# Source rows in a graph kernel: 2, 3, 2, 3 chunks per group fetched by TensorE, the rest gathered by GpSimd, in four passes over the edges

## The reference, cut to what matters

```python
# network 0, layer l
msg = h[src] * edge_weight[:, None]
h_neigh = segment_sum(msg, dst, num_segments=n) * inv_deg
h = h @ W_self[l].T + h_neigh @ W_neigh[l].T + b_neigh[l]
# network 1, layer l (h was scaled by norm_out)
m = h[src] * (a_mu + exp(a_ls) * eps)      # eps: 64 numbers for each edge
agg = segment_sum(m, dst, num_segments=n)
h = agg * norm_in @ W + b
```

## Time and profile before

| | us |
|---|---|
| runs, median of 3 | 11286.28 (11276.57 to 11294.67) |
| profiled execution, time | 11292.81 |
| its span | 11291.0 |
| mean granted TensorE clock | 0.711 of full speed |
| TensorE matmul busy | 7355.7 (65%) |
| VectorE busy | 7439.4 (66%) |
| GpSimd busy | 5284.9 (47%) |
| ScalarE busy | 3043.3 (27%) |

### The profile page before, as it was taken

The page is one execution under the profiler, slowest core; times in us unless marked ns, Lnnn a source line. Parts: engine busy times, 40 slices in busy tenths (PEclk is TensorE's granted clock), DMA queues, the critical chain, the costliest instruction groups (busy, mean ns, idle before and its releaser), DMA issues. The chain is left out here.

```text
span 11291.0 us, 165523 instructions
## 1 busy us (share of the span) xinstructions
PE 7355.7 (65%) x36229; PEld 5994.0 (53%) x36230; DVE 7439.4 (66%) x10348; ACT 3043.3 (27%) x11859; POOL 5284.9 (47%) x5319
## 2 busy tenths in 40 slices
PE   5777888777777765555477555555855555755557
PEld 4776888677777752323266222335733334633336
DVE  6666566555555556777899676779965556755558
ACT  1222455333333321111187111116910000000000
POOL 4555555444444427777300567750035553155650
PEclk8777999788888877667655676665565556855558
DMA  3333444344444437777488677766933333433333
GB/s 85 89 89 87 131 137 137 96 119 117 106 114 117 120 78 232 240 236 239 137 351 346 196 234 234 238 194 253 415 101 76 77 76 71 120 76 76 77 72 106
DMA packets 923105, 1720.96 MB, mean 152 GB/s; under 512 B 390554, under 2 KB 474359, under 8 KB 894105
## 3 DMA queue, kind: packets, MB, share of 16 engines
q1 hardware_dynamic: 666206, 1180.19, 30.8%
q0 software_dynamic: 196912, 401.32, 16.5%
q10 hardware_dynamic: 59904, 138.47, 3.2%
HBM read 1274.48 MB, written 444.85 MB: 152 GB/s over the span
## 5 line engine op out<-in xcount | busy, mean ns | idle before, releaser
L698 PE MATMUL ps_G<-table_parts,low_onehots 125*128 125x320 f32 x13520 | 2790.7, 372 | 621.7 <-DVE low_onehots L708 361.6
L535 POOL DMA_INDIRECT gathered_rows<-node_table,index x2184 | 2073.8, 950 | 1951.9 <-ACT index L525 858.5
L698 PEld LDWEIGHTS ps_G<-table_parts,low_onehots 125*128 125x128 f32 x13520 | 2563.9, 238 | 728.4 <-issue 579.0
L535 POOL DMA_INDIRECT gathered_rows<-xl_table,index x1664 | 1821.1, 1094 | 1656.1 <-PEq L1542 924.9
L535 POOL DMA_INDIRECT gathered_rows<-rel_table,index x1456 | 1380.2, 948 | 2052.6 <-ACT index L525 1114.4
L555 PE MATMUL ps_sum<-messages,onehots 128*125 128x65 f32 (+3 forms) x13312 | 1976.8, 313 | 426.3 <-issue 192.9
L1554 PE MATMUL ps_Z<-xr,onehots_wide 125*128 x3328 | 1477.1, 599 | 1113.9 <-issue 724.7
L555 PEld LDWEIGHTS ps_sum<-messages,onehots 128*125 128x125 f32 x13312 | 1899.0, 228 | 502.6 <-issue 502.0
L1554 PEld LDWEIGHTS ps_Z<-xr,onehots_wide 125*128 125x128 f32 x3328 | 779.9, 250 | 1811.1 <-issue 1694.2
L749 DVE TENSOR_TENSOR rows_by_feature<-ps_G,fifth_onehots 128x320 f32<-128x320 f32 x728 | 355.8, 489 | 1609.8 <-remote 1298.5
L1602 DVE TENSOR_TENSOR z<-gathered_rows,ps_Z 128x650 f32<-128x650 f32 x832 | 664.2, 828 | 768.2 <-issue 507.5
(11 more groups left out here) (328 smaller groups left out, 7830.5 us busy)
## 6 DMA issues: line engine op xcount, KB each, us to landing
stash_a<-gathered_rows SPq DMA_DIRECT2D x832, 325.0 KB
kept_rows<-stash_a SPq DMA_DIRECT2D x208, 1300.0 KB
onehots<-onehots_kept SPq DMA_DIRECT2D x520, 500.0 KB
onehots_turned<-onehots_turned SPq DMA_DIRECT2D x416, 256.0 KB
low_rows<-low_rows SPq DMA_DIRECT2D x312, 192.0 KB
stash_r<-gathered_rows ACTq DMA_DIRECT2D x208, 272.0 KB
kept_rows<-stash_r SPq DMA_DIRECT2D x208, 272.0 KB
onehots_kept<-onehots ACTq DMA_DIRECT2D x104, 500.0 KB
```

Source lines behind the costliest of these rows:

```text
L535: pool.indirect_dma_start(G[:, HALF * k + q, 0:width], None, table, bass.IndirectOffsetOnAxis(IDX[:, k, q:q + 1], 0)).then_inc(gathered[k] ...
L698: last = nc.tensor.matmul(ps_G[:, (fetch * k + g) % 2, 0:D * FIVE], OT[0:BN, k, g, a, :], HP[:, part, a, :, :].rearrange("p f b -> p (f b) ...
```

## The change

`FETCH_FIRST` (2) and `FETCH` (3) become plans by group of a turn, both (2, 3, 2, 3). So W0 fetches 10 chunks per turn in place of 8 and gathers 22 in place of 24; W1, A0 and A1 fetch 10 in place of 12 and gather 22 in place of 20. The counts of the semaphores follow the plan. SP's loop loads the low row of group n + 2 in step n, ahead of the wait for free chunks, the low rows of groups 0 and 1 before the loop; in A0 and A1 it issues the attributes ahead of the one-hots. The core of the diff:

```diff
-FETCH_FIRST = 2
-FETCH = 3
+FETCH_FIRST = (2, 3, 2, 3)
+FETCH = (2, 3, 2, 3)
...
-        def gather_loop(pool, G, width, table, IDX, free, count=HALF):
+        def gather_loop(pool, G, width, table, IDX, free, plan=(0,) * K):
...
-                    for q in range(count):
+                    for q in range(HALF - plan[k]):
...
+        def banks(plan, i, k):
+
+            return sum(plan) * i + sum(plan[:k])
+
-        def load_low_row(sp, LR, i, k, fetch=FETCH):
+        def load_low_row(sp, LR, i, k, plan):
+
+            i, k = i + k // K, k % K
+            f = plan[k]
             sp.wait_ge(low_made.sem, low_made.at(K * (i - 1) + k + 1))
-            sp.dma_start(LR[:, k, :], low_rows[bass.ds(K * i + k, 1), HALF - fetch:HALF, :].rearrange("o q c -> (o q c)").partition_broadcast(P)
+            sp.dma_start(LR[:, k, 0:f * P], low_rows[bass.ds(K * i + k, 1), HALF - f:HALF, :].rearrange("o q c -> (o q c)").partition_broadcast(P)
                          ).then_inc(low_loaded[k].sem, 16)
...
-                        with sp.Fori(0, TURNS) as i:
+                        def turn(i, last_turn):
                             for k in range(K):
+                                if not (last_turn and k >= K - 2):
+                                    load_low_row(sp, LR, i, k + 2, plan)
                                 if not hist:
                                     chunks_free(sp, i, k)
                                     load_onehots(sp, S, i, k)
-                                load_low_row(sp, LR, i, k, fetch)
+
+                        for k in range(2):
+                            load_low_row(sp, LR, 0, k, plan)
+                        with sp.Fori(0, TURNS - 1) as i:
+                            turn(i, False)
+                        turn(TURNS - 1, True)
...
-                        with sp.Fori(0, TURNS) as i:
+                        def turn(i, last_turn):
                             for k in range(K):
+                                if not (last_turn and k >= K - 2):
+                                    load_low_row(sp, LR, i, k + 2, plan)
                                 chunks_free(sp, i, k)
-                                load_onehots(sp, S, i, k)
-                                load_low_row(sp, LR, i, k)
                                 load_attributes(sp, mybir.EngineType.SP, i, k, 0)
                                 load_attributes(sp, mybir.EngineType.SP, i, k, HALF // 2)
+                                load_onehots(sp, S, i, k)
```

More of the change, by code:

```diff
@@ L712, in make_low_onehots, with mask_banks @@
                             ALU.is_equal).then_inc(high_made.sem, 1)
[L714 to L719, removed]
+        def mask_banks(act, HI, BR, ps_G, i, k, plan):
+            i, k = i + k // K, k % K
+            m, at = banks(plan, i, k), sum(plan[:k])
+            act.wait_ge(high_made.sem, high_made.at(K * i + k + 1))
+            for g in range(plan[k]):
+                act.wait_ge(row_picked.sem, row_picked.at(m + g - 1))
+                act.wait_ge(bank_made.sem, bank_made.at(m + g + 1))
@@ L720, in mask_banks @@
                 for b in range(FIVE):
[L721 to L722 removed]
+                    last = nc.scalar.activation(BR[:, (at + g) % 2, :, b],
+                                                ps_G[:, (at + g) % 2, 0:D * FIVE].rearrange("p (f b) -> p f b", b=FIVE)[:, :, b],
                                                 ACT.Copy, scale=HI[:, k, g, b:b + 1])
@@ L724, in mask_banks, with add_banks @@
                 last.then_inc(bank_picked.sem, 1)
-        def add_banks(dve, BR, G, i, k, fetch=FETCH):
+        def add_banks(dve, BR, G, i, k, plan):
             i, k = i + k // K, k % K
-            n = K * i + k
+            m, at = banks(plan, i, k), sum(plan[:k])
             chunks_free(dve, i, k)
-            for g in range(fetch):
-                dve.wait_ge(bank_picked.sem, bank_picked.at(fetch * n + g + 1))
-                nc.vector.tensor_reduce(G[:, HALF * k + HALF - fetch + g, :], BR[:, (fetch * k + g) % 2, :, :], AX, ALU.add).then_inc(row_picked.sem, 1)
@@ L735, in pick_rows @@
-        def pick_rows(dve, HI, BR, ps_G, G, i, k, fetch=FETCH, rows_of=None):
+            for g in range(plan[k]):
+                dve.wait_ge(bank_picked.sem, bank_picked.at(m + g + 1))
+                nc.vector.tensor_reduce(G[:, HALF * (k + 1) - plan[k] + g, :], BR[:, (at + g) % 2, :, :], AX, ALU.add).then_inc(row_picked.sem, 1)
+        def pick_rows(dve, HI, BR, ps_G, G, i, k, plan, rows_of=None):
             i, k = i + k // K, k % K
-            n = K * i + k
+            m, at = banks(plan, i, k), sum(plan[:k])
@@ L759, in picks_over @@
             for c in (bank_made, bank_picked, row_picked):
-                c.over(fetch * GROUPS)
+                c.over(sum(plan) * TURNS)
             table_split.over(1)
@@ L765, in weighted_sums @@
             phase[0] += 1
-            fetch = FETCH_FIRST if hist else FETCH
+            plan = FETCH_FIRST if hist else FETCH
             es = ExitStack()
@@ L938, in _ @@
                                              skip_group_check=True).then_inc(finished, 1)
-                for c in gathered:
-                    c.over(16 * (HALF - fetch) * TURNS)
+                for c, f in zip(gathered, plan):
+                    c.over(16 * (HALF - f) * TURNS)
                 chunk_done.over(NCH)
@@ L946, in weighted_sums @@
                     c.over(16 * TURNS)
-                picks_over(fetch)
+                picks_over(plan)
         def attribute_sums(AGG, attr, mu, spread, norm_in):
             phase[0] += 1
+            plan = FETCH
             es = ExitStack()
@@ L1079, in attribute_sums @@
                     c.over(16 * TURNS)
-                for c in gathered:
-                    c.over(16 * (HALF - FETCH) * TURNS)
+                for c, f in zip(gathered, plan):
+                    c.over(16 * (HALF - f) * TURNS)
                 for c in attr_loaded:
```

124 lines of the change are left out of this document (63 added, 61 removed).

## The result

The changed kernel takes 11441.74 us (median of 4 runs, 11406.17 to 11476.1), the kernel before beside it 11289.12: a ratio of 1.0134, interval 1.0103 to 1.0165. It is slower by 1.3%: by 153 us in the medians, and by 113 us in the two profiled executions (11406.17 against 11292.81; span 11404.4). The forecast was +101.

What follows compares the result with a forecast made beforehand. Gather runs holding TensorE's signals bound W0 and W1, SyncE's issuing A0 and A1. W0 -47 - 2.5, W1 +71 + 2.5, A0 and A1 2 x (42 + 2.5 - 6) = +77: +101 on 11286.3, 11387 us; range 11195 to 11465.

Steps and rivals of the forecast that it cites:

- What bounds the passes: W0, W1: TensorE's signals held from 4 us into a gather run until 1.4 us after; A0, A1: SyncE's issuing.
- Rival C: All passes: gathers hold nothing back, extra gathers are free; 0 to +59 us, 11286 to 11345; chance 0.10.
- W1, +71 and 2.5 for the start: W1: 52 groups with a sixth gather cost 1.36 us each, +71; longer first run +2.5; bounds 0 and +94.
- W0, -47 and -2.5: W0: two gathers fewer per turn gain 47 us, bounds -65 and +50; shorter first run gains 2.5.
- 35 to 36 were the sign of being right: W0: the profile after would show 35 to 36 us per turn, against 37.6 before.
- two gathers fewer: W0: leaving out two gathers per turn saves 1.8 to 2.5 us per turn, -47 to -65 over 26.
- so it just fits: W0: with two more fetched chunks per turn TensorE is busy 7.7 to 8.2 of 8.9 us per group, some loss.
- with one pair joined: W0: a turn with one pair of groups still gathered in one run takes 35.1 us in place of 37.6.
- Rival E: W0: TensorE becomes the bound, +50 in place of -50, GpSimd gaps exceed 3.7 us; 11487; chance 0.10.
- A0 and A1: 0.8 us for the sixth gather, +42 each: A0, A1: a sixth gather slows SyncE's issuing by 0.8 us in 52 groups, +42 per pass, bounds +20 and +65.
- SyncE's 10.1 us per group: A0: the profile after would show SyncE's queue still without waits, at 10.1 us per group.
- The order of the loads, -6 per A pass: A0, A1: VectorE's low-row waits become attribute waits; only the end of each pass gains, some 6 us.

Runs made afterwards that it cites:

- the second profile: The unchanged changed kernel measured again against the kernel before: 11195.38 against 11084.33 us, ratio 1.0098.
- the fetches alone: Kernel before; in W0 TensorE fetches a third chunk in odd groups while GpSimd still starts six gathers in every group: W0 1022.8 us (+27).
- the kernel with half of the attributes: Kernel before; in A0 and A1 SyncE loads attributes of four chunks per group, not eight: A0 868.6, A1 873.4 us (-112, -103).
- the version put together: Kernel before with new plan and three PSUM banks in W0, new load order, half of A0/A1 attributes from ScalarE's queue: 10963.36 us, ratio 0.9888.

## Why the prediction was right or wrong, step by step

- **What bounds the passes.** Right. That TensorE's signals are held while gathers run was the reading on which all rests; W1's period went from 8.2 to 9.49 us with the sixth gather, the gap unchanged and TensorE running on. Rival C is out. The reading has an end that the prediction did not have: with four gathers TensorE itself is the bound. And a run of eleven or twelve holds less strictly than "until about 1.4 us after its end".
- **W1, +71 and 2.5 for the start.** Right: +70, and +72 in the second profile. Neither the fetches taken away (a gain of 0, as said) nor the clock, which fell from 0.94 to 0.84, changed it.
- **W0, -47 and -2.5.** Wrong, +41 in its place, and 39.0 us per turn where 35 to 36 were the sign of being right. The half "two gathers fewer" was right, -56 alone. The failed step is "so it just fits": it compared TensorE's busy time with the period (8.0 of 8.9 us), as if the third chunk were only work. It is a wait as well. With two chunks and two banks TensorE hardly needed VectorE's answer inside a group (2.4 us of such waits in 800); with three it does, and when the answer comes late in a joint run, the chain fetch, pick, histogram, sums is left for the gap: 9.5 us in place of 3.65. The rows of the changed kernel and the two kinds of joint run with the fetches alone show this; no run takes away the wait and nothing else. The joint run that I counted as a gain (35.1 us per turn "with one pair joined") was the loss. 16 x (9.5 - 3.65) = 94 us is about the miss of 90 (all gaps above 0.5 us together: 222 us before, 322 after). Rival E gave the right size, +50, and the right sign to look for (gaps above 3.7 us), with a cause that the rows don't bear out: TensorE was busy 77% of W0 and stood still for up to 9.7 us behind the second chunk.
- **A0 and A1: 0.8 us for the sixth gather, +42 each.** The size was right where it could be taken apart: +38. In the first measurement it was not seen (+2 and +7 with the order's gain), and SyncE's 10.1 us per group did not come. The reading behind it (SyncE issues, it never waits) is borne out by the kernel with half of the attributes and by the version put together.
- **The order of the loads, -6 per A pass.** Mis-sized: -16 to -19. I allowed a gain only at the end of a pass, since SyncE never waits; its period fell from 9.16 to 8.99 us all the same. Why SyncE, which issues the same ten DMAs, then takes less wasn't found. In the first measurement the two terms together were +2 and +7 where the later runs had +16 and +20; there the order must have given more or the plan cost less. Neither half was run alone there, so this stays open.
- **The sum.** 101 was near 113 by luck: W0 came out 90 us above its term and the A passes 68 below theirs. The medians differ by 153, not 113: the profiled execution is the fastest of four that lie 70 us apart. In the kernel before three runs lie within 18 us. W0 alone showed 1041.6 and 1001.7 in two profiles; that it is also what varies from run to run is likely and not shown.
- **Open.** Why VectorE's first pick comes 5 to 9 us into most joint runs with the fetches alone and 11 to 16 us into those of the changed kernel; what holds the signals; a third bank with the positions left in PSUM (there is no bank free); a gather loop that pauses by itself inside a run.

## What to carry to other kernels

Where an engine that sends signals works beside a run of back-to-back indirect DMAs, price a change by the length of the run and by how many answers must cross it, not by busy shares, until the run is so short that the other engine is the bound. One more answer (for a third chunk on two banks) costs little while it comes early in the run, and the whole chain when it comes late. When an edit needs a second one to be possible (a bank freed by moving a tile), run that second one alone before believing the first. And add up a prediction by stage against the trace: two wrong terms can make a right sum.

## What the runs showed of the hardware that I had not expected

- Moving one operand of VectorE's comparisons from PSUM to SBUF leaves VectorE's time (1189 and 1192 ns) and lengthens the gathers beside it from 0.946 to 1.28 us in the mean, up to 2.9; and a pass can be faster by it (1001.7 to 912.4 us) or slower (882.7 to 923.1).
- TensorE's records for the same work in W1 sum to 706 to 815 us, at a granted clock of 0.99 to 0.88. By the Trainium skill's Trainium Architecture — The Big Picture, "What this means for kernel authors", one engine doesn't block another without a semaphore; one gather more per group made W1 142 us longer while GpSimd had 2.3 us to spare in each, so for the delivery of the signals the measurement decides against that sentence.
- The kernel before takes 11084 to 11116 us on three chips (medians) and 11289 and 11307 where it ran first and last; whether that is the chip isn't shown. Of the four passes those that SyncE bounds differ most: A0 980 against 1022 us and A1 976 against 1017, but W1 874 against 883 and W0 996 against 1001. A per-pass comparison across measurements misleads there by more than the edits are worth.
